# Two chained attention layers: in second-layer steps ScalarE's exponential of a unit and the logarithm are issued ahead of the exponential of the late fill

## The reference

```
# layer 0, per image x: (128, 1024)
theta, phi, g = W_theta x + b, W_phi x + b, W_g x + b
y = softmax(theta^T phi, axis=-1) g^T          # (1024, 128), then reshaped to (128, 1024) as it lies
z = (1 - w) x + w (W_z y + b_z)
# layer 1, per image z
q, k, v = Wq z + bq, Wk z + bk, Wv z + bv      # q and k have 16 channels
out = v softmax(q^T k / 4, axis=-1)^T
fused = Wf [gamma * out ; z] + bf              # the output
```

## Time and profile before

| | |
|---|---|
| median of 3 runs | 525.61 us (524.16 to 527.09) |
| the profiled execution: its time, its span | 525.3 us, 523.5 us |
| busy share of the span: TensorE matmul, weight load | 96%, 79% |
| VectorE, ScalarE, GpSimd | 77%, 68%, 59% |
| late fills' exponentials (L753, `fulls`) | 40, 1.024 us mean |
| units' exponentials (L730) | 128, 1.09 to 1.12 us mean, and 0.21 us to read the row sum |

### The profile page before, as it was taken

One profiled execution on the slowest core, in us unless ns is written; L12 is line 12 of the kernel. 1 busy time (PEld: TensorE's weight loads), 2 busy tenths in 40 slices (PEclk: granted clock), 3 DMA queues, 4 the chain that ended last, 5 costly groups with the idle time before them and its releaser, 6 DMA issues.

```text
span 523.5 us, 7901 instructions
## 1 busy us (share of the span) xinstructions
PE 501.3 (96%) x2647; PEld 413.0 (79%) x2647; DVE 403.2 (77%) x553; ACT 356.3 (68%) x619; POOL 307.7 (59%) x342
## 2 busy tenths in 40 slices
PE   7898999979999999999999999999999998899996
PEld 5686877858878888888888888888888886777886
DVE  4968685597779977898779968898779867876973
ACT  4756467568775787758785687758785578656763
POOL 1454255667579556966679565975679503744432
PEclk9998999999999999999999999999999999999999
DMA  5010000011000300003000210003000100000001
GB/s 186 17 40 3 0 16 0 2 34 56 8 22 1 100 15 22 2 1 109 8 22 1 92 26 0 21 3 108 10 20 2 40 29 8 2 29 28 22 20 42
DMA packets 18506, 15.30 MB, mean 29 GB/s; under 512 B 12918, under 2 KB 13474, under 8 KB 18466
## 3 DMA queue, kind: packets, MB, share of 16 engines
q1 hardware_dynamic: 18322, 14.67, 9.4%
q10 hardware_dynamic: 144, 0.13, 0.1%
HBM read 8.98 MB, written 4.24 MB: 25 GB/s over the span
## 4 chain that ended last, share of the span: by engine, by line
PE 82%; DVE 6%; ACT 5%; DMA 5%; issue 2%; SPq 0%; POOL 0%; DVEq 0%; ACTq 0%
PE trans L560 12%; PE accum L599 10%; PE accum L601 10%; PE accum L600 10%; PE scores L517 5%; PE scores L543 5%; PE scores L519 5%; PE scores L518 5%; PE trans L570 4%; PE misc L517 3%; PE misc L519 3%; PE misc L518 3%; PE misc L626 3%; DMA turned<-shift_parts 2%; DMA x_keep<-x_dram 1%
## 5 line engine op out<-in xcount | busy, mean ns | idle before, releaser
L882 DVE TENSOR_REDUCE neg_max<-scores 128x1 f32<-128x1024 f32 x128 | 155.3, 1214 | 4.5 <-PE scores L543 3.4
L746 ACT ACTIVATE pt_hi<-trans 128x512 fp32r<-128x512 f32 x168 | 91.8, 597 | 73.1 <-PE trans L560 67.8
L892 DVE TENSOR_TENSOR pt_lo<-trans,pt_hi 128x512 fp32r<-128x512 f32 x168 | 107.8, 682 | 32.3 <-ACT pt_hi L746 30.9
L730 ACT ACTIVATE fulls<-scores,neg_max 128x1024 f32<-128x1024 f32 x84 | 94.3, 1123 | 9.5 <-DVE neg_max L882 9.5
L560 PE MATMUL trans<-ident,fulls 128*128 128x128 f32 x672 | 89.2, 275 | 7.0 <-ACT fulls L730 1.9
L560 PEld LDWEIGHTS trans<-ident,fulls 128*128 128x128 f32 x672 | 75.8, 141 | 18.6 <-ACT fulls L730 6.9
L599 PE MATMUL accum<-pt_hi,g_hi 128*128 128x512 f32 x176 | 70.6, 401 | 1.1 <-DVE o_sb L960 1.0
L601 PE MATMUL accum<-pt_hi,g_lo 128*128 128x512 f32 x176 | 69.1, 393 | 0.0
L600 PE MATMUL accum<-pt_lo,g_hi 128*128 128x512 f32 x176 | 69.0, 392 | 0.0
L899 DVE TENSOR_TENSOR pt_lo<-fulls,pt_hi 128x1024 fp32r<-128x1024 f32 x40 | 53.8, 1345 | 6.3 <-POOL pt_hi L1078 5.2
L1078 POOL CAST pt_hi<-fulls 128x1024 fp32r<-128x1024 f32 x40 | 45.7, 1142 | 20.0 <-ACT fulls L753 19.9
(11 more groups left out here) (186 smaller groups left out, 1041.1 us busy)
## 6 DMA issues: line engine op xcount, KB each, us to landing
x_keep<-x_dram SPq DMA_DIRECT2D x8, 512.0 KB, 3.3
out_dram<-o_sb SPq DMA_DIRECT2D x15, 256.0 KB, 2.0
x_raw<-x_tiles_dram SPq DMA_DIRECT2D x7, 512.0 KB, 3.6
k_op<-qk_op SPq DMA_DIRECT2D x16, 96.0 KB, 2.3
x_raw<-x_tiles_dram SPq DMA_DIRECT2D x2, 256.0 KB, 3.7
turned<-shift_parts SPq DMA_DIRECT2D x22, 2.0 KB, 8.5
w_all<-weights_t_dram SPq DMA_DIRECT2D x1, 336.0 KB, 3.9
out_dram<-o_sb SPq DMA_DIRECT2D x2, 128.0 KB, 1.8
```

The costliest lines, as they stand in the source:

```text
L730: nc.scalar.activation(result, scores[:, k % 2, :], ACT.Exp, bias=neg_max[:, k % 16:k % 16 + 1], accum_out=row_sum[:, slot(gb), t:t + 1]). ...
L746: nc.scalar.activation(pt_hi[:, side(gb), 4 * bank:4 * bank + 4, t * P:(t + 1) * P], trans[:, cols(bank)].rearrange("p (n q) -> p n q", n= ...
L882: nc.vector.tensor_reduce(neg_max[:, k % 16:k % 16 + 1], scores[:, k % 2, :], AX.X, ALU.max, negate=True).then_inc(max_ready, 1)
L892: nc.vector.tensor_tensor(pt_lo[at], trans[:, cols(bank)].rearrange("p (n q) -> p n q", n=4), f(pt_hi[at]), ALU.subtract).then_inc(pt_lo_r ...
```

## The change

In `emit` of ScalarE the loop over the late fills (but block 24's) moves from the head of the step to behind the unit's exponential and the logarithm. It stays ahead of the small groups, but for a phi group where `first` is true, which is now ahead of it. No instruction, buffer, semaphore or wait is added or taken away, and no other engine's order changes.

```diff
                 before, after = SCHEDULE[k]
-                for gb, j in late_fills(k - 1):
-                    if gb != ASIDE:
-                        late_exp(gb, j)
                 if 0 <= k - 2 < UNITS and (k - 2) // TPB in TURNED:
                     unit_hi(k - 2)
                 first = bool(before and after and before[0][0] == "phi" and (k - 1) // TPB in LATE)
...
                     gb, t = divmod(k - 1, TPB)
                     if gb in LATE and t % 2:
                         pair_log(gb, t // 2)
+                for gb, j in late_fills(k - 1):
+                    if gb != ASIDE:
+                        late_exp(gb, j)
                 if not first:
                     for group in before:
                         small(group)
```

## The result

The changed kernel takes 544.2 us (median of 4 runs, 543.38 to 546.71), the kernel before beside it 524.88 us (median of 4 runs, 523.66 to 527.09). The ratio is 1.034 with a 95% interval of 1.030 to 1.039: slower by some 19 us. The profiled execution took 543.38 us with a span of 541.6 us, 18.1 us longer than before.

What follows compares the result with a forecast made beforehand. TensorE was taken to bound the kernel, with no idle time to give back. Five pairs of blocks at 2.86 + 0.8 us add 18.3 us to 525.3, plus 0.3 for the median: 543.9, said as 544, range 533 to 549.

Steps and rivals of the forecast that it cites:

- TensorE has no slack: Over the late blocks TensorE's matmuls are busy 283.61 of 285 us, so each delay reaching its queue stays.
- The rival by which the busy record overstates the load: TensorE makes up 3.66 us a pair from slack: no change, 525.6 us; chance 0.05.
- Kind A, the stall at fill 1: In five blocks with phi's copy ahead of the unit's exponential, fill 0 ends late; TensorE stalls 1.42 us.
- Kind A, GpSimd's train: GpSimd's gapless instructions from `late_hi` to the split of y move 2.86 us, delaying TensorE's f and z equally.
- the lower bound: Kind A costs only 1.42 us a block if GpSimd's train is shorter in the new order.
- Kind B: Five blocks without phi ahead: 0.8 us each at TensorE's transposes through fill 2, including 0.25 at fill 1.
- The 0.81 us saved beside VectorE: Kind B: the train's first `late_hi` no longer runs beside VectorE's `late_lo`, so 0.81 us comes off 1.59.
- The sum: Five pairs of blocks, each 2.86 + 0.8 = 3.66 us, give 18.3 us; bounds 8.4 and 22.3.
- The signs: Expected in the profile after: given TensorE waits, unchanged busy times, one pair growing from 59.6 to about 63.2 us.
- Direct stalls only: TensorE loses only 1.42 and 0.25 us a pair, GpSimd and VectorE absorb the rest: 534 us; chance 0.16.
- More contention: GpSimd and VectorE hinder each other as much or more, kind B costs 1.6 us: 548 us; chance 0.14.
- Faster by the score buffers: Scores wait for earlier units' exponentials, so 0.57 us comes off each kind B block: 522.8 us; chance 0.03.

Runs made afterwards that it cites:

- the split put first: The change, with GpSimd's phi split ahead of `late_hi` in the five kind A steps with fill 0: 536.45 us, beside 525.66 for the kernel before.
- the copy put behind: The change, but in five steps the phi copy comes behind the late fill, not ahead of the unit's exponential: 533.01 us, beside 527.5 for the kernel before.
- kind A alone: The change made only in the five blocks where a phi copy precedes the unit's exponential: 539.81 us, beside 527.5 for the kernel before.

## Why the prediction was right

The forecast was 544 us, the measurement 544.2. The mechanism held, but that the number is so near is partly luck. The two sizes are off by 0.2 us a block in opposite directions. And the kernel before came out at 524.88 us where the sum started from 525.6, so that the measured difference is 19.3 us and not 18.3.

**TensorE has no slack.** Right. Whatever reached its queue stayed: after the last late block the kernel was 18.0 us late and remained so (block 24's fill 0 is issued at 435.96 before and 453.95 after). The rival by which the busy record overstates the load, the reading of the Trainium skill's page Perfetto Trace Analysis (section Identifying the Most-Contended Engine), fell: with weight loads busy 83% there was nothing to make up 3.6 us in 60. The 83% is what a full engine shows here: a load of 0.19 us in a pitch of 0.23. The little slack that there is, is what TensorE already waited, such as the 0.28 us for y; it took up 0.1 us in two of the experiments.

**Kind A, the stall at fill 1: 1.42 us.** From block 10's fill 0 to fill 1 TensorE takes 215.88 - 210.99 = 4.89 us, before 209.99 - 206.59 = 3.40 (that fill 0's issue is at 206.59 in the kernel before): 1.49. The term that was too small is the signal. The prediction put 0.05 us between the fill's end and TensorE's next issue, which is what GpSimd needs (215.73 to 215.79); TensorE takes 0.15 (215.73 to 215.88, and in block 8 184.05 to 184.20).

**Kind A, GpSimd's train: 2.86 in all.** `late_hi` of fill 0 is 215.79 - 208.55 - 4.40 = 2.84 us late, the 4.40 being TensorE's lateness at that point (210.99 - 206.59). The f group is 223.56 - 216.48 - 4.40 = 2.68 us late. The train took 12.02 us (215.79 to 227.81) where it had 12.19, so a little of it shrank, as the lower bound had allowed: VectorE's `late_lo` now runs beside the split of phi and no longer beside the shift. Over the block it is 2.64 where the sum had 2.86. That the train carries the second part, and the phi copy's wait the first, was argued in the prediction; the split put first and the copy put behind have shown it.

**Kind B: 0.8.** It is 0.98. Fill 1 lost 0.32 and not 0.25, again by the signal, and TensorE another 0.11 before qk, so that ScalarE got to the exponential of unit 43 later than I had it. `late_hi` of fill 2 was late by 190.56 - 185.43 = 5.13 less the 3.37 of TensorE (180.70 - 177.33), 1.76 us instead of 1.6. The 0.81 us saved beside VectorE are there: `late_hi` took 1.04. And `late_hi` of fill 3 starts 196.54 - 192.22 - 3.37 = 0.95 us late. The prediction held against itself that `late_lo` of fill 2 "then runs beside the split of x". It misread the kernel before, where the two met already:

```profile
188.12 1.22 DVE L899 TENSOR_TENSOR pt_lo<-fulls,pt_hi 128x1024 fp32r<-128x1024 f32 x1
...
188.35 3.25 POOL L1013 TENSOR_TENSOR x_lo<-x_raw,x_hi 128x1024 fp32r<-128x1024 f32 x1
```

`x_lo` takes 3.25 us before and after. What is new is that `late_lo` starts with 0.7 us of `x_hi` still to run (0.15 before) and stretches to 1.76 us.

**The sum.** Five pairs at 3.6 make 18.1, and the first pair, near 117 to 150 us, lost a little less, 3.5. In it lies the wait for the shift's DMA, 1.3 us before and 0.6 after; as the longest such wait is 1.0 to 2.4 us in the other nine profiles, the difference needn't come from the change. Predicted 18.3, measured 18.1 in the span.

**The signs.** TensorE waits 1.3 us for `late_exp` five times and 0.2 to 0.3 five times, f waits for y, the transposes wait 2.7 us in five blocks for `pt_lo`, and the stretch of one pair on ScalarE is 277.97 - 214.73 = 63.24 us, where 63.2 was said. The granted clock stayed at 1.00. Only the busy times did not stay as they were: VectorE's `late_lo` has 57.2 us in place of 53.8, GpSimd's `late_hi` 41.6 in place of 45.7.

**The rivals.** Direct stalls only: out, by kind A alone and by GpSimd's split put first. More contention: out in kind B, see above. Faster by the score buffers: TensorE shows no wait for a unit's exponential in the late blocks before or after; the exponentials came earlier and nothing took it up.

## What to carry to other kernels

When an instruction is moved behind another, look at what that other one waits for, and not only at what it costs. The same 1.2 to 1.3 us of work ahead of the fill cost, by the losses per block, nothing in 25 fills, half a microsecond in ten, and 2.6 us in the five where a copy that waits for TensorE stood ahead of it too. Then follow the late result through each in-order queue that it feeds, and ask for each whether it has a gap before its next deadline: here GpSimd, 59% busy over the kernel, had none for 12 us.

## What the runs showed of the hardware

TensorE's clock can make a wait cost more than its length. In the kernel with only kind B's fill 0 moved, TensorE was idle over half of the 4 us around its wait for the late landing, and the granted clock of the next 5 us was 0.66 on average, between its two levels of 1.2 and 2.4 GHz (columns as in the earlier trace rows):

```profile
195.00:200.00 5.00, 5.00 (x29) 4.06 (x28) 4.69 (x7) 3.30 (x6) 2.42 (x3) 1.00 0.04 5
200.00:204.00 4.00, 1.72 (x12) 1.41 (x11) 1.31 (x3) 2.18 (x4) 1.37 (x2) 1.00 0.00 0
204.00:209.00 5.00, 5.00 (x20) 4.12 (x19) 1.62 (x3) 1.65 (x3) 1.88 (x2) 0.66 0.01 1
```

The wait was 2.3 us, and 4.1 us were lost in that place. The clock accounts for the rest: an estimate from the row is 5 us x (1 - 0.66) = 1.7 us. In the second profile of that kernel the wait was 1.2 us, the granted clock stayed at 1.00, and 1.4 us were lost. In the changed kernel twenty waits of TensorE's matmuls, of 0.2 to 1.3 us each, left the clock at 1.00 in every 5 us from 115 to 420 us.

GpSimd and VectorE hold each other up where VectorE subtracts two tensors of the state buffer (SBUF). Beside `late_lo` the rounding of 128x1024 took 1.85 us and 1.04 without, and the shift of two columns about 1.0 to 1.2 us and 0.19. By the Trainium skill, GPSIMD Engine Reference, section Specifications, GpSimd's interfaces to that memory are shared with VectorE, with contention when VectorE's instruction has two inputs there; the trace agrees.

Which of the two pays can be read from the rows: the one that starts second, and it pays what the other still has to run. In the kernel before, `late_lo` starts at 188.12 and `x_lo` at 188.35; `late_lo` takes its 1.22 us and `x_lo` 3.25. With x rounded a step early `x_lo` starts first, at 187.98, and takes 2.40; `late_lo`, from 188.85, takes 2.61. In all eleven profiles every one of the 40 `late_lo` between 117 and 420 us fits this within 0.15 us, and so does every GpSimd instruction that starts beside one. So a change of order alone can move 0.8 us or more from one engine to the other.
